# A 16-batch attention kernel with experts: splits on VectorE, thinner scatters, clearing from ScalarE's queue, overlapped expert pairs, and logits in pairs

## The reference

```python
x = x + conv_attention(group_norm(x))       # 8 heads, 768x768 scores per batch, two bias
                                            # tables, causal over T, softmax, projection Wo
t = x.reshape(16, 768, 128)
# additive attention on layer_norm(t)
A = q @ W1[:, :e].T + b1;  B = k @ W1[:, e:].T             # 16 hidden channels
hidden = tanh(A[:, :, None, :] + B[:, None, :, :])         # (16, 768, 768, 16)
logits = einsum('bijh,h->bij', hidden, w2) + b2
t = t + softmax(logits) @ v
# mixture of experts on layer_norm(t): 12288 tokens, the best 2 of 8 experts,
# at most 1920 tokens an expert, in the order of the tokens
probs = softmax(xf @ gate_w.T); topk_vals, topk_idx = top_k(probs, 2)
h = gelu(expert_in @ w1 + b1, approximate=False);  expert_out = h @ w2 + b2
t = t + sum of the two experts' rows, weighed by the normalised topk_vals
```

## Time and profile before

| | |
|---|---|
| median of 3 runs | 2494.8 us (2486.47 to 2506.36) |
| the profiled execution's own time | 2480.88 us, of it the span of the trace 2479.1 |
| mean clock of TensorE over the span | 0.937 |
| TensorE busy | 2074.1 us (84%) |
| ScalarE busy | 1679.3 us (68%) |
| VectorE busy | 1581.9 us (64%) |
| GpSimd busy | 1535.1 us (62%) |

### The profile page before, as it was taken

The page is one execution under the profiler, slowest core; times in us unless marked ns, Lnnn a source line. Parts: engine busy times, 40 slices in busy tenths (PEclk is TensorE's granted clock), DMA queues, the critical chain, the costliest instruction groups (busy, mean ns, idle before and its releaser), DMA issues.

```text
span 2479.1 us, 56587 instructions
## 1 busy us (share of the span) xinstructions
PE 2074.1 (84%) x17665; PEld 1131.1 (46%) x17665; DVE 1581.9 (64%) x4438; ACT 1679.3 (68%) x1933; POOL 1535.1 (62%) x1590
## 2 busy tenths in 40 slices
PE   2887798989898889888889898889899876548887
PEld 1343444444444444444444444444445443236766
DVE  5775577776667677767676777677767555323333
ACT  4236687878677777777777787778778878513332
POOL 3015565757575757575757575757575768637677
PEclk7898999999999999999999999999999999769999
DMA  3643422222222222232323232222221000025553
GB/s 77 106 87 84 116 46 59 53 59 54 58 54 57 57 57 55 50 58 49 63 50 62 51 60 50 52 57 49 55 42 32 11 5 6 5 57 80 81 80 38
DMA packets 145200, 137.87 MB, mean 56 GB/s; under 512 B 24473, under 2 KB 135798, under 8 KB 144816
## 3 DMA queue, kind: packets, MB, share of 16 engines
q1 hardware_dynamic: 119376, 109.87, 21.8%
q0 software_dynamic: 25504, 24.14, 5.7%
HBM read 82.68 MB, written 54.12 MB: 55 GB/s over the span
## 4 chain that ended last, share of the span: by engine, by line
PE 35%; DVE 18%; issue 16%; POOLq 10%; POOL 7%; DVEq 6%; ACT 4%; DMA 2%; SPq 1%; ACTq 0%
PE logits L959 10%; POOLq L788 9%; DVE max_halves L1244 4%; POOL hidden L789 4%; PE ring L1033 3%; POOL out_dram L565 3%; PE ring L1055 2%; PE av_bank L945 2%; PE scores L929 2%; PE scores L932 2%; PE ring L1047 2%; ACT hidden L887 2%; PE logits L468 2%; ACT hidden L885 2%; DVE logit_bias L1419 1%
## 5 line engine op out<-in xcount | busy, mean ns | idle before, releaser
L789 POOL TENSOR_SCALAR hidden<-b_rep,a_cols 128x768 f32<-128x768 f32 x1152 | 1048.5, 910 | 433.8 <-issue 289.3
L885 ACT ACTIVATE hidden<-hidden 128x2304 f32<-128x2304 f32 x384 | 817.1, 2128 | 262.5 <-POOL hidden L789 262.4
L959 PE MATMUL logits<-hidden,w_shifted 128*32 128x384 f32 x6144 | 611.4, 518 | 171.6 <-ACT hidden L887 128.3
L1244 DVE TENSOR_REDUCE max_halves<-ring 128x1 f32<-128x384 f32 (+4 forms) x896 | 471.4, 549 | 244.8 <-PE ring L1033 243.6
L862 ACT ACTIVATE probs<-scores 128x512 f32<-128x512 f32 (+1 forms) x768 | 384.4, 541 | 230.4 <-PE scores L932 229.6
L959 PEld LDWEIGHTS logits<-hidden,w_shifted 128*32 128x32 f32 x6144 | 167.3, 113 | 433.7 <-issue 230.6
L887 ACT ACTIVATE hidden<-b_rep,a_cols 128x768 f32<-128x768 f32 x384 | 357.6, 931 | 0.0
L1033 PE MATMUL ring<-k_max,q_max 112*128 112x384 bf16 (+4 forms) x1024 | 296.6, 320 | 11.9 <-DVE max_halves L1244 6.0
L929 PE MATMUL scores<-bias_q,onehot_k 112*128 112x512 bf16 (+1 forms) x768 | 277.6, 362 | 23.9 <-ACT probs L862 18.4
L932 PE MATMUL scores<-q_parts,k_parts 98*128 98x256 bf16 (+1 forms) x1536 | 279.5, 264 | 0.0
L821 POOL DMA_INDIRECT expert_rows<-rows,slots x192 | 191.4, 997 | 80.5 <-DVE slots L1392 42.8
(11 more groups left out here) (260 smaller groups left out, 2624.7 us busy)
## 6 DMA issues: line engine op xcount, KB each, us to landing
qk_parts<-qk_parts_sb SPq DMA_DIRECT2D x16, 1152.0 KB, 4.3
q_parts<-qk_parts SPq DMA_DIRECT2D x192, 96.0 KB, 3.8
k_parts<-qk_parts SPq DMA_DIRECT2D x192, 96.0 KB, 4.6
q_max<-qk_parts SPq DMA_DIRECT2D x96, 96.0 KB, 3.0
k_max<-qk_parts SPq DMA_DIRECT2D x96, 96.0 KB, 3.7
expert_rows<-clear_row POOLq DMA_DIRECT2D x10, 792.0 KB, 5.4
x_in<-in_x_dram SPq DMA_DIRECT2D x96, 64.0 KB, 2.2
x<-in_x_dram SPq DMA_DIRECT2D x96, 64.0 KB, 2.3
```

What stands on the lines that cost most here:

```text
L789: last = g.tensor_scalar(hidden[:, q % SLOTS, o, :], b_rep[:, side], 1.0, a_cols[:, side, a_col(q, o):a_col(q, o) + 1], ALU.mult, ALU.add)
L885: s.activation(hidden[:, t % SLOTS, 0:3, :], hidden[:, t % SLOTS, 0:3, :], ACT.Tanh)
L959: last = mm(logits[32 * g:32 * g + 32, half, 0:HALF], w2_shifted[:, k, :], hidden[:, q % SLOTS, g, HALF * half:HALF * half + HALF], start= ...
L1244: v.tensor_reduce(max_halves[:, h:h + n_, part], bank[:, 0:n_ * keys].rearrange("p (h k) -> p h k", h=n_), AX.X, ALU.max, negate=True).the ...
```

## The change

Five things are changed.

1. The second and third parts of q and k are made by VectorE, in six pieces: a cast of 768 columns and two subtractions of 384 columns each for q (tick 14, slots 1 to 3) and for k (tick 16, slots 0 to 2). SyncE's store of the parts moves from tick 15 to tick 17.
2. GpSimd sends half of the twelve scatters in ticks 18 to 23 and the other half in ticks 0 to 5 of the next pass, one a tick. In the pass without `mid` (the last one with `add`) it sends three in ticks 18 to 23, and the other nine in the pass after it. In the first pass with `add`, which has no `end` batch before it, it sends none in ticks 0 to 5. Two tables are preset so that the early scatters of the first `end` hit nothing. GpSimd drains its pipeline between the sums only in passes with `max`, and before the first sum only in ticks 7 to 18.
3. One of the ten clearing DMAs is issued by GpSimd in its preparation, and nine by ScalarE, between the two Tanh instructions of every second tick from 1 to 17.
4. TensorE adds the logits of two groups in every second tick, in slot 0.
5. In the expert stage a pair's last products stand behind the first transposes of the next pair. The weights of the first two experts are loaded before the rows are complete, and later weights behind an expert's second chunk of rows.

```diff
-SPLIT_AT = (11, 13)
-SEND_FROM = 15
+SPLIT_AT = ((14, 1), (16, 0))
+SEND_FROM, SENDS = 18, 12
-CLEAR_AT = tuple(range(1, 20, 2))
-CLEARS = len(CLEAR_AT)
+CLEAR_AT = tuple(range(1, 19, 2))
+CLEARS = 1 + len(CLEAR_AT)
...
         def expert_pairs(eng, body):
-            body(0, 0)
-            with eng.Fori(1, E // 2) as pair:
-                body(pair, pair * 2)
+            body(0, 0, False)
+            with eng.Fori(1, E // 2 - 1) as pair:
+                body(pair, pair * 2, False)
+            body(E // 2 - 1, E - 2, True)
...
-            sp.wait_ge(rows_sent, 16 * CLEARS + 192 * NB)
+            sp.wait_ge(av_done, 24 * NB)
             sp.sem_inc(sp_passed, 1)
+            for r in range(2):
+                load_weights(r, r)
+            sp.wait_ge(rows_sent, 112 + 192 * NB)
+            sp.sem_inc(sp_passed, 1)
...
-                for n in range(2 * CHUNKS + 1):
-                    if n == 0:
-                        transpose_rows(0)
-                    if n + 1 < 2 * CHUNKS:
-                        transpose_rows(n + 1)
-                    if n < 2 * CHUNKS:
-                        up(n)
-                    if n > 0:
-                        down(n - 1)
+            def body(pair, e0, last_pair):
+                if not positive(e0):
+                    transpose_rows(pair, e0, 0)
+                for n in range(2 * CHUNKS):
+                    if n + 1 < 2 * CHUNKS or not last_pair:
+                        transpose_rows(pair, e0, n + 1)
+                    up(pair, e0, n)
+                    if n or positive(e0):
+                        down(e0, n - 1)
+                if last_pair:
+                    down(e0, 2 * CHUNKS - 1)
...
                 for o in range(3):
-                    if o or 0 < q <= SEND_FROM:
+                    if ps.has("max") and (o or TICKS - SEND_FROM < q <= SEND_FROM):
                         pool.drain()
...
+            def sends(ps):
+                if ps.has("add"):
+                    return SENDS // 2 if ps.has("mid") else SENDS // 4
+                return SENDS
...
-                        if not positive(ps.batch("add")) and t in CLEAR_AT:
-                            clear_rows(CLEAR_AT.index(t))
...
-                            g.tensor_copy(qk_parts[:, w, 1, :], qk_rest[w])
-                            pool.drain()
-                            g.tensor_tensor(qk_parts[:, w, 2, :], qk_rest[w], qk_parts[:, w, 1, :],
-                                            ALU.subtract).then_inc(parts_ready, 1)
...
+            def clear_rows(k):
+                if k == 1:
+                    act.wait_ge(made, 5)
+                act.dma_start(cleared[k], clear_source).then_inc(rows_cleared, 16)
...
                         s.activation(hidden[:, t % SLOTS, 0:3, :], hidden[:, t % SLOTS, 0:3, :], ACT.Tanh)
+                        if not positive(b) and t in CLEAR_AT:
+                            clear_rows(1 + CLEAR_AT.index(t))
...
-                    stage, q = ("add", t - 1) if t else ("end", TICKS - 1)
+                    stage, q = ("add", t - 2) if t else ("end", TICKS - 2)
                     for slot in range(PARTS):
-                        if slot == 0 and q % 4 and ps.has(stage):
+                        if slot == 0 and t % 2 == 0 and ps.has(stage) and q >= 0:
                             add_logits(ps.batch(stage), q)
+                            add_logits(ps.batch(stage), q + 1)
...
-                        if slot == 2 and q % 4 == 0 and ps.has(stage):
-                            add_logits(ps.batch(stage), q)
...
+            def split(w, k):
+                dve.drain()
+                if k == 0:
+                    v.tensor_copy(qk_parts[:, w, 1, :], qk_rest[w])
+                else:
+                    cols = slice(HALF * (k - 1), HALF * k)
+                    last = v.tensor_tensor(qk_parts[:, w, 2, cols], qk_rest[w][:, cols], qk_parts[:, w, 1, cols],
+                                           ALU.subtract)
+                    if k == 2:
+                        last.then_inc(parts_ready, 1)
```

236 lines of the change are left out of this document (121 added, 115 removed).

## The result

The changed kernel took 2476.7 us (median of 20 runs, 2460.5 to 2497.8). The kernel before took 2498.8 us in the runs beside it (19 of them from 2483.9 to 2515.8, and one of 3626.4 that counts as slow and is left out of the ratio). The ratio is 0.9905, with a 95% interval of 0.9879 to 0.9931. So the change is worth about 24 us, not 162, and the time lies above the range of 2275 to 2405.

The account below looks back on a forecast made before the run. TensorE had the most work, but GpSimd, late after waiting for VectorE, paced the full passes. Terms -86, -30, -32, -12, -3 and +1 summed to -162: 2480.88 became 2319, forecast 2332 us as median, range 2275 to 2405.

Parts of the forecast that it names:

- The pairs: Full pass, two groups' logits every second tick: 0.1 us a pair, 1.2 us a pass added.
- rival (d): Paired logits leave VectorE three banks and starve the ring: up to 1.5 us a pair, about 2550 us; chance 0.04.
- the softmax chain stays as long as it was: Full pass, paired logits: a block's last group is still added at the start of the tick divisible by four.
- The splits: Full pass: 10.6 us gained from removed waits and lower clock, 2.2 us of VectorE's six pieces on the path.
- the 2.08 us gap at the pass's start: TensorE's gap where the next pass begins: goes because GpSimd, without its splits, has three ticks' lead.
- The exclusion: VectorE's six pieces and GpSimd's operations exclude each other: 0 to 3.8 us of waiting, middle taken, 6 us VectorE time.
- Pass 0: Nine clearings move to ScalarE's queue at 0.5 us each: -30 us, bounds -15 and -36.
- The tail: Passes 13, 14 and 15, thin scatters and fewer drains: -6, -14 and -12, together -32 us, bounds -18 and -40.
- six softmax maxima at 1 us: Passes 14 and 15: ScalarE becomes the bound and waits 6 us for the maxima, giving 90 and 80.5 us.
- The expert stage: Expert scatters: 244 us where 255.80 stood, -12 us, bounds -7 and -16; the gain is GpSimd's, not TensorE's.
- Start of the experts: First expert rows issued ahead of weight loads, 1.4 us earlier and beside less traffic: -3 us, 0 to -4.
- rival (a): VectorE becomes the bound: a full pass gains 3 us and not 7.2, total 2382 us; chance 0.20.

Follow-up runs that it names:

- a_spread: The changed kernel with the second group of logits in slot 2 of the same even tick, not directly behind the first: 2509.9 us.
- a_single: The changed kernel with the pairs undone, TensorE adding one group of logits a tick: 2384.1 us, ratio 0.958.
- b_split: The kernel before with only the splits moved to VectorE's six pieces and SyncE's store in tick 17: 2439.6 us, ratio 0.981.
- as_nopieces: a_single without VectorE's six pieces from batch 1 on, output wrong: 2386.2 us.
- one-sum runs: GpSimd makes only the last of three sums from batch 1 on, output wrong: 2286.3 us against a_single's edit base, 2323.6 us in the changed kernel.

## Why the prediction was wrong, step by step

**The pairs: the step that failed most.** "I take 0.1 us a pair, 1.2 a pass", on the ground that "the mean need ... leaves room for catching up". Measured: 4.5 us a pass in the kernel before and 7.8 in the changed one, 53 and 92 us in all. That is rival (d), "the pairing starves the ring", with its place and sign right and its mechanism only half right. It gave 0 to 1.5 us a pair, and 7.8 a pass is 0.65 a pair, not the 1.1 at which it would have decided alone. But a_spread shows that it is not the three banks during the 3 us. It is what the odd ticks lack. A mean need over a pass says nothing about a stretch like that from 1233.4 to 1246.8 us, in which VectorE waits for no other engine. The sentence "the softmax chain stays as long as it was" was wrong in its argument too: the block's last two groups are added in one go at the start of the tick, so its maximum comes after 3 us of logits and not after 1.5. ScalarE waits for VectorE 6.0 us a pass in the changed kernel, where it was 4.7.

**The splits.** "Gain 10.6" and "on the path I take 2.2" made 8.4. Measured: 3.2 for the splits alone, and 3.5 with the thinner scatters and all the rest but the pairs (126.1 against a_single's 122.6). The gap of 4.5 us and the lower clock behind it did go (7.2 us in b_split). The pieces, for which I took 2.2, cost nothing that can be seen (as_nopieces). The term for "the 2.08 us gap at the pass's start" was wrong in its cause and its count. In the twelve full passes such a gap stands only where the hardware loop of two passes turns, five times in all, of 2.1 to 2.5 us before and of 2.0 to 2.5 us in the changed kernel. It is no wait for GpSimd, and it stays. And what the view of before couldn't show came on top: with GpSimd ahead, its instructions fall together with VectorE's rows of tick 19. In a_single, TensorE's timeline of a pass in which they met and of one in which they hardly did:

```profile
774.37 0.54 PE L1037 MATMUL ring<-ident,heads 128*128 128x128 f32 x3 [2.11 <-DVE heads L1217]
...
777.43 1.64 PE L1066 MATMUL ring<-headsT,map_b 128*128 128x384 f32 x2 [1.08 <-DVE headsT L1291]
...
1261.82 0.54 PE L1037 MATMUL ring<-ident,heads 128*128 128x128 f32 x3 [0.34 <-DVE heads L1217]
...
1264.89 0.91 PE L1066 MATMUL ring<-headsT,map_b 128*128 128x384 f32 x2 [1.48 <-DVE headsT L1291]
```

VectorE's three rows took 2.09 us there, beside a scatter and a sum, and 0.97 here. That is 1.1 us, and ticks 20 to 22 took 15.4 and 11.4 us. Most of the rest is the lower clock after the gap: the granted clock is 0.66 from 775 to 785 us, and the same two matmuls take 1.64 us where they take 0.91. It is so in all the passes: in the six in which these rows met GpSimd (the first of them 1.07 to 1.08 us), the stretch took 14.5 to 16.3 us, and in five of the other six 11.4 (13.1 in one).

**The exclusion.** The prediction cited it, priced it for the six new pieces alone (2 us of 6), and wrote that it "matters little once GpSimd has a lead". The price belonged as much to VectorE's normalised rows and its operations on seven columns, all from SBUF to SBUF. By the one-sum runs two of three sums are worth 6.2 us a pass in a_single and 11.4 with the pairs. With the pairs it is larger than any single term of the sum, and it was in the kernel before already (VectorE's rows of tick 6 have a median of 0.53 us there).

**Pass 0** was forecast at -30 and is -35.5: the issues on ScalarE's queue took 0.38 to 0.43 us. Two of the nine:

```profile
189.47 0.43 ACTq L870 DMA_DIRECT2D expert_rows<-clear_row  x1
...
196.83 0.38 ACTq L870 DMA_DIRECT2D expert_rows<-clear_row  x1
```

**The tail:** -32 forecast, -5.4 measured. In the last pass with sums ScalarE's wait for GpSimd is gone (it was 17.8 us in pass 15), and its wait for the softmax maxima has taken its place. Waits of ScalarE from 2075.1 to 2164.9 us:

```profile
ACT probs L886 <- DVE logit_bias L1448: 18.4, 6, 9.3
```

The term "six softmax maxima at 1 us" was mis-sized: 3.1 us in the mean, one of them 9.3. The pairs have little part in it: pass 15 takes 88.2 us in a_single. With two of three sums left out the wait is 7.9 us and the pass 79.3 us without pairs and 78.3 with them, near the 80.5 of the forecast, and pass 14 takes 88.8 and 88.7 us, near its 90. So it is mostly the sums' hindrance, and the rows say that the change itself made it worse there: it took the drains between the sums out. No run puts them back. VectorE's small operations ahead of the wait of 9.3 us, and GpSimd's sums beside them:

```profile
2094.46 0.81 DVE L1125 TENSOR_SCALAR ln_small<-ln_small 128x7 int32<-128x7 int32 x1
2095.35 0.79 DVE L1128 SCALAR_TENSOR_TENSOR ln_small<-ln_small 128x7 f32<-128x7 f32 x1
...
2095.02 10.79 POOL L803 TENSOR_SCALAR hidden<-b_rep,a_cols 128x768 f32<-128x768 f32 x12
```

All ten of these operations on seven columns take 0.79 to 0.81 us. In pass 15 of the kernel before, with 0.17 us between one sum and the next, every second one got through:

```profile
2080.69 0.75 DVE L1110 SCALAR_TENSOR_TENSOR ln_small<-ln_small 128x7 f32<-128x7 f32 x1
2081.52 0.17 DVE L1112 TENSOR_TENSOR ln_small<-ln_small 128x7 f32<-128x7 f32 x1
```

Pass 13 was to lose 6 us and lost none. It takes 115.4 us in a_single, and 107.9 and 109.6 with the sums thinned out, without pairs and with them.

**The expert stage** was right in size and in reason: -13.7 for -12. TensorE's gaps of 7.69 us are gone (three waits for that copy made 22.9 us, and six make 8.1 now, the longest 2.3). GpSimd still idles at each expert:

```profile
2268.87 1.54 POOL L583 DMA_INDIRECT out_dram<-x_in,probs  x1 [3.46 <-DMA out_dram<-x_in,headsT]
```

**Start of the experts:** from the last Tanh to the first scatter, the kernels with the earlier loads take 65.7 to 68.0 us and those without 68.7 to 70.1, as forecast, but for four in which the last softmax came late (70.7 to 73.2 us, one of them the changed kernel, below). The nine put-off scatters cost nothing, as the prediction said.

Of its tests, GpSimd's wait before a cast is gone and the clearings take under 1 us, as forecast. The pass is not 117 to 121 us but 130, and 9 of its 288 groups of logits still take over 2.2 us (15 before). TensorE's waits on VectorE grew by 7.5 us, just under the 8 of "over 8 would be (a) or (d)". The chance of 0.04 for (d) was far too low. Without the pairs the kernel comes out at 2384 us, where rival (a), VectorE as the bound, gave 2382. Its full pass (3 us gained, 3.5 measured) and its reason are near. That the totals agree is luck: passes 13 to 15 of a_single gained 5 us and not 32.

## What to carry to other kernels

Work that does not need the result of the engine that lags is what covers its lag. Moving it out of a stretch uncovers every wait there, even where the mean load leaves room. Before you free an engine, look at what runs beside it now and will be hindered: here two of GpSimd's three sums hindered VectorE by 6.2 us a pass, and by 11.4 with the pairs, where GpSimd's own stall in ticks 14 to 16 had cost 7.2, and making GpSimd wait for two of VectorE's stretches gained 24 us. Price such an edit by the busiest tick, not by the pass.
